# One attention phase in another order on all its engines, with splits and fills one turn later and other PSUM banks for the units

## The chip, the core and the metric

The program runs on one core of one Trainium2 chip. The core has five engines that run their own instruction streams side by side: PE (TensorE, matmuls), DVE (VectorE), ACT (ScalarE), POOL (GpSimd) and SP (SyncE, which here issues DMAs). They order their work between them by semaphores. The metric is the device time of the whole program in microseconds (us); lower is better.

## What is computed

The program computes four layers in a row on x of shape (32, 256, 128): a retention layer, a mixture of experts, an attention layer, and a routed decoder block. The change touches the third, and the bookkeeping of x around it:

```
# 16 heads of 8 values each, 32 sequences of 256 tokens
def _L1_attn_ref(hidden_states, Wq, bq, Wk, bk, Wv, bv, Wo, bo):
    q = (hidden_states @ Wq.T + bq).reshape(b, s, HEADS, HEAD_DIM)
    k = (hidden_states @ Wk.T + bk).reshape(b, s, HEADS, HEAD_DIM)
    v = (hidden_states @ Wv.T + bv).reshape(b, s, HEADS, HEAD_DIM)
    q = q * SCALE
    scores = jnp.einsum('bqhd,bkhd->bhqk', q, k)
    probs = jax.nn.softmax(scores.astype(jnp.float32), axis=-1)
    out = jnp.einsum('bhqk,bkhd->bqhd', probs, v).reshape(b, s, d)
    return out @ Wo.T + bo
...
x = x + _L1_attn_ref(_layernorm(x), ...)
```

## The kernel before

**The phase.** `attention_phase` (L1008) works on the 32 sequences one after the other, as a software pipeline. Each engine has its own list of steps with a lag each, handed to `pipeline` (L55): in turn n of that engine, a step with lag g works on sequence n - g. Rounds 0 to 9 are written out, rounds 10 to 31 run in a hardware loop whose body holds two turns, and the rest is written out again. Engines stay in step only by semaphores, so turn n of one engine need not lie at the same time as turn n of another.

**One sequence.** DVE takes statistics of x (`stats_of`, `moments`), POOL makes the factors from them (`inv_std`), ACT normalises (`norm`), PE transposes h (`transpose_h`) and projects q and k (`project_qk`, L1546), ACT copies them out of PSUM (`copy_qk`). To keep f32 precision with bf16 matmuls, POOL splits q and k into three bf16 parts each: `split_qk(0)` and `split_qk(1)`, four instructions each (L1234), every one waiting for the one before. SP stores the parts (`store_parts`, four DMAs) and reads them back into the stacks of one half of the heads (`fill(0)`, `fill(1)`, two DMAs each). PE then computes scores twice. `for_maximum(j)` (m0 to m7, L1460) writes a unit of 4 heads x 128 queries x 256 keys into one of three PSUM slots of two banks each, and DVE takes the row maxima from there (`maximum(j)`, L1319). POOL splits the maxima (`split_max(half)`, four small instructions), PE transposes them (`transpose_max`, L1528), ACT copies them (`copy_maxT`), and SP puts them below the queries (`give_max(half)`). `for_exponential(j)` (e0 to e7, L1476) computes the transposed scores less the maximum into a slot, and ACT takes the exponential (`exponential(j)`, L1406). `values(g)` (L1491) multiplies with v. Then come `copy_o`, `by_token` (L1539), `normalise`, `transpose_o`, `output`, `add_y`, and a second set of statistics with `inv_std3`, `norm3`, `weigh`, `add_up` and `store_out` for the next layer. `pad_v`, `bias` and `add_given` are further steps of POOL.

**What sets the order.** The lists of steps are written by hand, one for each engine. `UNITS` names the 16 units in PE's order, with their lag and slot; before PE writes a slot it waits until DVE or ACT has read the unit that was there (`free_slot`). `TURNS` gives the order in which eight small products share the one bank `ps_misc` (v, oT, y, max1, hT, token, qk, max0): each waits until the one before it is read (`misc_free`).

The lists before, in short: POOL `inv_std3 8, bias 5, inv_std 1, weigh 9, split_max(0) 4, add_given 0, pad_v 4, split_qk(0) 2, split_qk(1) 2, split_max(1) 4`; PE begins its turn with e4 and `values(1)`, and m and e units stand mostly in pairs.

## Time and profile before

| | us |
|---|---|
| median of 3 runs | 1094.35 (1092.17 to 1096.04) |
| the profiled execution, device time | 1095.34 |
| its span, first to last instruction | 1093.6 |
| mean granted TensorE clock | 0.944 of 2.4 GHz |

The time of an execution is 1.74 us more than the span of its trace, for what lies around the instructions. The attention phase takes about 458 to 988 us of the span. Its steady part is a row of turns of some 15 us, one for each sequence; the length of a turn is read from the distance between two starts of the same line, for instance L1539, which runs once a turn. In the trace, "idle before <-releaser" names what ended an engine's wait.

### The profile page before, as it was taken

The numbers are of one execution on the slowest core, as the hardware profiler recorded it, in microseconds if no ns is written. First come the engines' busy times: TensorE is split into PE (matmuls) and PEld (weight loads), VectorE is DVE, ScalarE is ACT, GpSimd is POOL, SyncE is SP. The second block draws the span as 40 slices with busy tenths as digits, with TensorE's granted clock in tenths as the row PEclk, the third lists the DMA queues.
The fourth block names the chain that finished last, engine by engine and source line by source line (L and its number), as shares of the span: only waits on it lengthen the run. The fifth ranks groups of instructions, "written<-read, shape, count | busy, mean of one in ns | idle before, by whom it ended". The sixth has DMA issues, their size and how long they took to land. (4 is left out here: it accounts for less than half of the span.)

```text
span 1093.6 us, 31502 instructions
## 1 busy us (share of the span) xinstructions
PE 978.4 (89%) x9858; PEld 715.5 (65%) x9858; DVE 710.5 (65%) x1509; ACT 642.1 (59%) x1320; POOL 707.5 (65%) x1531
## 2 busy tenths in 40 slices
PE   6999999699989999359999999999999999973776
PEld 5888888489956766235766666666666666642554
DVE  5777777685534444235777888777887778735752
ACT  4666766412223443115788888888888788762552
POOL 4666676467735555456688888888888888635003
PEclk9999999799989999756999999999999999996988
DMA  8500000131123332363344444344444344302000
GB/s 321 246 0 0 0 0 0 40 106 54 50 72 82 84 81 66 92 192 92 112 118 138 120 133 125 117 120 135 115 131 120 112 134 122 112 16 65 12 3 20
DMA packets 84095, 99.99 MB, mean 91 GB/s; under 512 B 10590, under 2 KB 68158, under 8 KB 83646
## 3 DMA queue, kind: packets, MB, share of 16 engines
q1 hardware_dynamic: 78782, 87.97, 27.0%
q0 software_dynamic: 5248, 11.15, 3.2%
q8 instruction: 41, 0.67, 0.3%
q14 instruction: 24, 0.20, 0.1%
HBM read 61.78 MB, written 36.47 MB: 90 GB/s over the span
## 5 line engine op out<-in xcount | busy, mean ns | idle before, releaser
L1319 DVE TENSOR_REDUCE a_neg_max<-a_slot 128x4 f32<-128x1024 f32 x256 | 301.6, 1220 | 89.8 <-PE a_slot L1460 88.2
L1406 ACT ACTIVATE a_pT<-a_slot 128x1024 f32<-128x1024 f32 x256 | 255.6, 1026 | 16.1 <-PE a_slot L1476 14.5
L1476 PE MATMUL a_slot<-a_q_stack,a_k_stack 75*128 75x256 bf16 x1024 | 156.7, 276 | 3.9 <-issue 1.7
L1460 PE MATMUL a_slot<-a_k_stack,a_q_stack 72*128 72x256 bf16 x1024 | 149.8, 281 | 9.0 <-DMA a_k_stack<-part_dram 6.9
L1491 PE MATMUL a_ps_o<-a_pT,a_v_pad 128*32 128x256 f32 x2048 | 138.1, 387 | 0.0
L1460 PEld LDWEIGHTS a_slot<-a_k_stack,a_q_stack 72*128 72x128 bf16 x1024 | 93.5, 100 | 50.9 <-issue 22.0
L702 POOL DMA_INDIRECT y_rows<-m_total,m_token x80 | 76.6, 957 | 67.2 <-ACT m_total L855 53.3
L1476 PEld LDWEIGHTS a_slot<-a_q_stack,a_k_stack 75*128 75x128 bf16 x1024 | 91.7, 98 | 34.4 <-DVE a_neg_max L1319 10.1
L325 DVE TENSOR_TENSOR r_score<-ps_score,r_decay 128x512 f32<-128x512 f32 x128 | 81.5, 678 | 10.1 <-PE ps_score L477 10.0
L1491 PEld LDWEIGHTS a_ps_o<-a_pT,a_v_pad 128*32 128x32 f32 x2048 | 53.6, 109 | 48.4 <-issue 26.3
L695 POOL DMA_INDIRECT sorted_in<-h,m_slot x64 | 63.9, 998 | 26.1 <-issue 18.6
L804 DVE TENSOR_TENSOR m_hidden_e<-m_gate_e,m_banks 128x512 f32<-128x512 f32 x40 | 27.5, 687 | 77.4 <-ACT m_gate_e L850 77.4
L934 PE MATMUL m_banks<-expert_up,m_xeT 128*128 x160 | 77.4, 607 | 0.0
L885 PE MATMUL m_banks<-h2T,shared_up 128*128 (+1 forms) x256 | 61.9, 386 | 2.2 <-DVE m_hidden L751 1.9
L380 ACT ACTIVATE r_h<-x,r_shift,r_rstd 128x128 f32 (+1 forms) x128 | 56.7, 498 | 9.3 <-POOL r_shift L252 9.3
L835 ACT ACTIVATE m_gate<-m_banks 128x512 f32<-128x512 f32 x32 | 19.1, 597 | 66.7 <-PE m_banks L885 66.7
L850 ACT ACTIVATE m_gate_e<-m_banks 128x512 f32<-128x512 f32 x40 | 23.9, 597 | 55.3 <-PE m_banks L934 55.3
L885 PEld LDWEIGHTS m_banks<-h2T,shared_up 128*128 128x128 f32 x256 | 47.2, 194 | 8.8 <-issue 3.4
L1234 POOL TENSOR_TENSOR a_part<-a_qk,a_zeros 128x256 bf16<-128x256 f32 x64 | 39.1, 611 | 16.6 <-ACT a_qk L1392 14.1
L250 POOL TENSOR_TENSOR r_rstd<-r_ve,r_half 128x2 f32<-128x2 f32 x64 | 45.3, 707 | 6.0 <-POOL r_minus_mean L247 1.9
L1234 POOL TENSOR_TENSOR a_part<-a_rest,a_part 128x256 bf16<-128x256 f32 x64 | 42.9, 671 | 5.0
L1234 POOL TENSOR_TENSOR a_rest<-a_qk,a_part 128x256 f32<-128x256 f32 x64 | 42.8, 669 | 5.0
(292 smaller groups left out, 2132.4 us busy)
## 6 DMA issues: line engine op xcount, KB each, us to landing
a_q_stack<-part_dram SPq DMA_DIRECT2D x64, 288.0 KB
a_k_stack<-part_dram SPq DMA_DIRECT2D x64, 288.0 KB
part_dram<-a_part SPq DMA_DIRECT2D x64, 192.0 KB, 2.7
sorted_in<-h SPq DMA_DIRECT2D x10, 528.0 KB, 14.0
m_xe<-sorted_in SPq DMA_DIRECT2D x40, 132.0 KB, 2.3
expert_up<-in_eu_dram SPq DMA_DIRECT2D x1, 4096.0 KB, 25.7
part_dram<-a_part SPq DMA_DIRECT2D x64, 64.0 KB, 3.5
out_dram<-e_x_plus_h SPq DMA_DIRECT2D x32, 128.0 KB, 1.8
```

The lines of the kernel that those rows point to most:

```text
L325: nc.vector.tensor_tensor(score[:, p, tile], ps_score[tile][:], own, ALU.mult).then_inc(score_done, 1)
L380: ins = nc.scalar.activation(h[:, p, t], x_sb[:, s * TPS + t, :], ACT.Identity, bias=shift[:, p, t:t + 1], scale=rstd[:, p, t:t + 1])
L695: nc.gpsimd.indirect_dma_start(sorted_in, bass.IndirectOffsetOnAxis(ap=slot[:, t:t + 1], axis=0), h2_all[:, t, :], None).then_inc(scattere ...
L702: nc.gpsimd.indirect_dma_start(y_rows, bass.IndirectOffsetOnAxis(ap=token[:, at:at + 1], axis=0), ye[:, t % RING, j], None).then_inc(store ...
L885: ins = nc.tensor.matmul(bank[2 * which + p][:, f * S:(f + 1) * S], shared_up[:, which, f], h2T_all[:, bass.ds(s * S, S)], start=True, sto ...
L934: ins = nc.tensor.matmul(bank[PAIR * (p % 2) + j], xeT[:, p % 2, j], w_up[:, expert[j]], start=True, stop=True)
L1234: nc.gpsimd.tensor_tensor(to, a, b, op).then_inc(steps, 1)
L1319: nc.vector.tensor_reduce(neg_max[:, p, half, t, g * UNIT:(g + 1) * UNIT], slots[SLOT_OF["m", j]][:], AX.X, ALU.max, negate=True).then_inc ...
L1406: nc.scalar.activation(pT[:, j % PT_RING], slots[SLOT_OF["e", j]][:], ACT.Exp).then_inc(e_read, 1)
L1460: ins = nc.tensor.matmul(slots[SLOT_OF["m", j]][:, q], q_stack[0:QK_ROWS, p, half, head, t * P:(t + 1) * P], k_stack[0:QK_ROWS, p, half, h ...
L1476: ins = nc.tensor.matmul(slots[SLOT_OF["e", j]][:, q], k_stack[0:EXP_ROWS, p, half, head, t * P:(t + 1) * P], q_stack[0:EXP_ROWS, p, half, ...
L1491: ins = nc.tensor.matmul(ps_o[q * APAD:(q + 1) * APAD, g // 2], v_pad[:, p, t, g * UNIT + q], pT[:, (2 * g + t) % PT_RING, q], start=g % 2 ...
```

## The change

All five lists and the tables `UNITS` and `TURNS` are rewritten. Lines below L1296 have numbers 2 or 3 higher in the changed kernel. No arithmetic step is added or removed.

- On PE the m and e units alternate, and the turn begins with e6. Every unit has its slot from the new `UNITS`.
- On POOL `split_qk` goes from lag 2 to 3, `split_max` from 4 to 5, `inv_std` from 1 to 2; `split_max(0)` stands first and `inv_std` stands between the two `split_qk`.
- On SP `store_parts` goes from lag 1 to 3, the fills from 2 to 3 and 4, and the list begins with `fill(1)`.
- On DVE the maxima m0 to m6 go from lag 3 to 4, `moments` from lag 0 to 1 and behind the fifth maximum; `given_added` waits for two semaphores more.
- On ACT exponentials and copies stand in a new order, with `norm3` at the end (lag 6, from 7).

```diff
-UNITS = (("e", 4, 5, 0), ("e", 5, 5, 2), ("m", 6, 4, 1), ("m", 7, 4, 0), ("e", 6, 5, 2), ("e", 7, 5, 1),
-         ("m", 0, 3, 2), ("m", 1, 3, 1), ("e", 0, 4, 0), ("e", 1, 4, 2), ("m", 2, 3, 0), ("m", 3, 3, 1),
-         ("e", 2, 4, 2), ("e", 3, 4, 0), ("m", 4, 3, 1), ("m", 5, 3, 2))
+UNITS = (("e", 6, 5, 2), ("m", 7, 4, 0), ("e", 7, 5, 1), ("m", 0, 3, 2), ("e", 0, 4, 1), ("m", 1, 3, 0),
+         ("e", 1, 4, 2), ("m", 2, 3, 1), ("e", 2, 4, 0), ("m", 3, 3, 2), ("e", 3, 4, 1), ("m", 4, 3, 0),
+         ("m", 5, 3, 2), ("e", 4, 4, 1), ("m", 6, 3, 0), ("e", 5, 4, 1))
...
-            pipeline(sp, [(give_max(1), 4), (store_out, 9), (fill(0), 2), (give_max(0), 3), (fill(1), 2),
-                          (store_parts, 1)], B, ROUNDS)
+            pipeline(sp, [(fill(1), 4), (store_parts, 3), (store_out, 9), (give_max(1), 5),
+                          (fill(0), 3), (give_max(0), 4)], B, ROUNDS)
...
-            pipeline(pool, [(inv_std3, 8), (bias, 5), (inv_std, 1), (weigh, 9), (split_max(0), 4), (add_given, 0),
-                            (pad_v, 4), (split_qk(0), 2), (split_qk(1), 2), (split_max(1), 4)], B, ROUNDS)
+            pipeline(pool, [(split_max(0), 5), (weigh, 9), (add_given, 0), (split_qk(0), 3), (inv_std, 2),
+                            (split_max(1), 5), (split_qk(1), 3), (bias, 5), (pad_v, 4), (inv_std3, 8)], B, ROUNDS)
...
             def given_added(s, p, r):
+                after(dve, stats_done, s - 1)
+                after(dve, ve_done, 2 * (s - 2))
                 after(dve, added, s + 1)
...
-            pipeline(dve, [(given_added, 0), (maximum(7), 4), (add_up, 9), (stats_of, 0), (moments3, 7),
-                           (maximum(0), 3), (maximum(1), 3), (settle, 0), (add_y, 6), (moments, 0),
-                           (maximum(2), 3), (maximum(3), 3), (normalise, 5), (y_is_added, 6), (maximum(4), 3),
-                           (maximum(5), 3), (stats3_of, 6), (maximum(6), 3), (settle3, 6), (preset_v_pad, 0)], B, ROUNDS)
+            pipeline(dve, [(given_added, 0), (maximum(0), 4), (add_up, 9), (add_y, 7), (maximum(1), 4),
+                           (maximum(2), 4), (moments3, 8), (stats_of, 0), (y_is_added, 7), (maximum(3), 4),
+                           (normalise, 6), (maximum(4), 4), (moments, 1), (stats3_of, 7), (maximum(5), 4),
+                           (settle3, 7), (maximum(6), 4), (settle, 0), (maximum(7), 4), (preset_v_pad, 0)], B, ROUNDS)
...
-            pipeline(act, [(norm3, 7), (exponential(3), 4), (copy_qk, 1), (exponential(4), 4), (copy_maxT(0), 3),
-                           (exponential(5), 4), (copy_v, 1), (copy_o(0), 4), (exponential(6), 4),
-                           (exponential(7), 4), (copy_oT, 5), (norm, 0), (exponential(0), 3), (exponential(1), 3),
-                           (copy_o(1), 4), (copy_maxT(1), 3), (copy_hT, 0), (exponential(2), 3)], B, ROUNDS)
+            pipeline(act, [(copy_qk, 1), (exponential(4), 4), (copy_maxT(0), 3), (copy_o(0), 4),
+                           (exponential(5), 4), (exponential(6), 4), (copy_v, 1), (exponential(7), 4),
+                           (copy_oT, 5), (exponential(0), 3), (norm, 0), (copy_maxT(1), 3), (exponential(1), 3),
+                           (copy_o(1), 4), (copy_hT, 0), (exponential(2), 3), (exponential(3), 3),
+                           (norm3, 6)], B, ROUNDS)
...
-            TURNS = (("max0", 4, maxT_copied, 2, 0), ("v", 2, v_copied, 1, 0), ("oT", 6, oT_copied, 1, 0),
-                     ("y", 6, y_added, 1, 0), ("max1", 4, maxT_copied, 2, 1), ("hT", 1, hT_copied, 1, 0),
-                     ("token", 5, otok_copied, 1, 0), ("qk", 1, qk_copied, 1, 0))
+            TURNS = (("v", 2, v_copied, 1, 0), ("oT", 6, oT_copied, 1, 0), ("y", 6, y_added, 1, 0),
+                     ("max1", 4, maxT_copied, 2, 1), ("hT", 1, hT_copied, 1, 0), ("token", 5, otok_copied, 1, 0),
+                     ("qk", 1, qk_copied, 1, 0), ("max0", 3, maxT_copied, 2, 0))
...
-            pipeline(pe, [(for_exponential(4), 5), (values(1), 5), (transpose_max(0), 4), (for_exponential(5), 5),
-                          (for_maximum(6), 4), (for_maximum(7), 4), (project_v, 2), (for_exponential(6), 5),
-                          (for_exponential(7), 5), (values(2), 5), (for_maximum(0), 3), (transpose_o, 6),
-                          (for_maximum(1), 3), (for_exponential(0), 4), (output, 6), (for_exponential(1), 4),
-                          (values(3), 5), (for_maximum(2), 3), (transpose_max(1), 4), (for_maximum(3), 3),
-                          (for_exponential(2), 4), (transpose_h, 1), (values(0), 4), (by_token, 5),
-                          (for_exponential(3), 4), (for_maximum(4), 3), (for_maximum(5), 3),
-                          (project_qk, 1)], B, ROUNDS)
+            pipeline(pe, [(for_exponential(6), 5), (project_v, 2), (for_maximum(7), 4), (for_exponential(7), 5),
+                          (values(2), 5), (for_maximum(0), 3), (transpose_o, 6), (for_exponential(0), 4),
+                          (for_maximum(1), 3), (output, 6), (for_exponential(1), 4), (for_maximum(2), 3),
+                          (transpose_max(1), 4), (values(3), 5), (transpose_h, 1), (for_exponential(2), 4),
+                          (for_maximum(3), 3), (for_exponential(3), 4), (by_token, 5), (values(0), 4),
+                          (for_maximum(4), 3), (project_qk, 1), (for_maximum(5), 3), (for_exponential(4), 4),
+                          (for_maximum(6), 3), (transpose_max(0), 3), (values(1), 4),
+                          (for_exponential(5), 4)], B, ROUNDS)

```

**POOL, in the hardware loop.** What stands there after the second `split_qk` and at the loop's jump. Rows without a tile (REGISTER_ALU, ISA, branches) are instructions that POOL's sequencer handles: they compute addresses and wait values. Semaphores are printed under the name of their first owner: r_k_tok_done counts the steps of `split_qk`, r_stats2_part those of `split_max`, r_x1_done is `maxT_done`, r_stats2_done is `m_read`. Before:

```order
L1234 TENSOR_TENSOR a_part<-a_rest,a_part 128x256 [waits r_k_tok_done]
L45 REGISTER_ALU
L45 REGISTER_ALU [waits r_k_tok_done]
L45 REGISTER_ALU [waits r_x1_done]
L1234 TENSOR_TENSOR a_max_part<-a_neg_max,a_zeros 128x2x8 [waits r_stats2_done]
...
L1234 TENSOR_TENSOR a_max_part<-a_max_rest,a_max_part 128x2x8 [waits r_stats2_part]
L67 REGISTER_ALU [waits r_stats2_part]
L67 COMPARE_AND_BRANCH
```

Now:

```order
L1234 TENSOR_TENSOR a_max_part<-a_max_rest,a_max_part 128x2x8 [waits r_stats2_part]
L1234 TENSOR_TENSOR a_part<-a_qk,a_zeros 128x256 [waits r_qk_done,r_stats2_part]
...
L1234 TENSOR_TENSOR a_part<-a_rest,a_part 128x256 [waits r_k_tok_done]
L45 REGISTER_ALU
L1205 ISA [waits r_shift1_done,r_k_tok_done]
L1205 TENSOR_TENSOR x<-x,a_bo 128x256
...
L1220 TENSOR_TENSOR e_shift<-e_minus_mean,e_rstd 128x2 [waits e_rstd_done]
L67 REGISTER_ALU
L67 COMPARE_AND_BRANCH
```

The second maximum split moved from behind the second `split_qk` to ahead of it, and the jump now follows `inv_std3` in place of a split.

**SP, in the hardware loop.** The stores of the parts (L1143, L1147) and the DMA that gives the maxima of the second half (L1166; r_ve2_done is `maxT_copied`). Before:

```order
L1147 DMA part_dram<-a_part 64x6x256 [waits r_k_tok_done]
L1147 DMA part_dram<-a_part 64x6x256
L45 REGISTER_ALU
L1166 DMA a_q_stack<-a_max_T 3x8x256 [waits r_ve2_done]
L45 REGISTER_ALU
L1173 ISA [waits e_out_done]
L1173 DMA out_0_dram<-e_x_plus_h 128x2x128
```

Now:

```order
L1147 DMA part_dram<-a_part 64x6x256 [waits r_k_tok_done]
L1147 DMA part_dram<-a_part 64x6x256
L45 REGISTER_ALU
L1173 ISA [waits e_out_done]
L1173 DMA out_0_dram<-e_x_plus_h 128x2x128
L45 REGISTER_ALU
L1166 DMA a_q_stack<-a_max_T 3x8x256 [waits r_ve2_done]
```

The output store now goes ahead of the maxima; how long the first row waits depends on POOL, whose second `split_qk` now ends later relative to `transpose_max(1)`.

**PE, the start of a turn.** The units m6, m7, e6, e7, `values(2)`, m0, m1 with their slots, before:

```order
L1460 MATMUL a_slot1<-a_k_stack,a_q_stack 128x256 x4
L1460 MATMUL a_slot0<-a_k_stack,a_q_stack 128x256 x4
L1552 MATMUL a_ps_misc<-a_wv,a_hT 128x128 x2
L1476 MATMUL a_slot2<-a_q_stack,a_k_stack 128x256 x4
L1476 MATMUL a_slot1<-a_q_stack,a_k_stack 128x256 x4
L1491 MATMUL a_ps_o<-a_pT,a_v_pad 32x256 x8
L1460 MATMUL a_slot2<-a_k_stack,a_q_stack 128x256 x4
```

Now, from e6 on (e6, v, m7, e7, `values(2)`, m0, e0):

```order
L1479 MATMUL a_slot2<-a_q_stack,a_k_stack 128x256 x4
L1555 MATMUL a_ps_misc<-a_wv,a_hT 128x128 x2
L1463 MATMUL a_slot0<-a_k_stack,a_q_stack 128x256 x4
L1479 MATMUL a_slot1<-a_q_stack,a_k_stack 128x256 x4
L1494 MATMUL a_ps_o<-a_pT,a_v_pad 32x256 x8
L1463 MATMUL a_slot2<-a_k_stack,a_q_stack 128x256 x4
L1479 MATMUL a_slot1<-a_q_stack,a_k_stack 128x256 x4
```

Before, e7 took slot 1 after m6 with only m7, v and e6 between. Now slot 1 goes from e7 to e0 with `values(2)` and m0 between, and m6 hands slot 0 to m7.

## Rows read from the trace of the kernel before

**Rows 1.** Stretch of 80 us: PE, PEld, DVE, ACT, POOL busy; clock; DMA share; GB/s.

```profile
640.00:720.00 80.00, 79.30 (x812) 54.78 (x809) 63.41 (x107) 65.23 (x113) 68.12 (x161) 1.00 0.43 124
```

**Rows 2.** Timeline of PE, one line (L1539) of five turns: start us, us, line.

```profile
521.47 0.66 PE L1539 MATMUL a_ps_misc<-ident,a_oT_pad 128*128 128x128 f32 x4
536.34 0.66 PE L1539 MATMUL a_ps_misc<-ident,a_oT_pad 128*128 128x128 f32 x4
...
865.78 0.66 PE L1539 MATMUL a_ps_misc<-ident,a_oT_pad 128*128 128x128 f32 x4
880.55 0.66 PE L1539 MATMUL a_ps_misc<-ident,a_oT_pad 128*128 128x128 f32 x4
895.92 0.66 PE L1539 MATMUL a_ps_misc<-ident,a_oT_pad 128*128 128x128 f32 x4
```

**Rows 3.** Timeline of POOL, its last wait and its next one at `split_qk(0)`.

```profile
569.90 0.61 POOL L1234 TENSOR_TENSOR a_part<-a_qk,a_zeros 128x256 bf16<-128x256 f32 x1 [0.56 <-ACT a_qk L1392]
...
929.51 0.61 POOL L1234 TENSOR_TENSOR a_part<-a_qk,a_zeros 128x256 bf16<-128x256 f32 x1 [1.99 <-ACT a_qk L1392]
```

**Rows 4.** Timeline of POOL: end of `split_max(1)`, start of `inv_std3`, then `bias`.

```profile
546.79 0.22 POOL L1234 TENSOR_TENSOR a_max_part<-a_max_rest,a_max_part 128x16 bf16<-128x16 f32 x1
547.09 0.20 POOL L1212 TENSOR_TENSOR e_ve<-e_mv,a_eps 128x2 f32<-128x2 f32 x1
...
863.09 0.22 POOL L1234 TENSOR_TENSOR a_max_part<-a_max_rest,a_max_part 128x16 bf16<-128x16 f32 x1
863.53 0.19 POOL L1212 TENSOR_TENSOR e_ve<-e_mv,a_eps 128x2 f32<-128x2 f32 x1 [0.22 <-POOL a_max_part L1234]
...
864.88 0.74 POOL L1205 TENSOR_TENSOR x<-x,a_bo 128x256 f32 x1
...
877.86 0.22 POOL L1234 TENSOR_TENSOR a_max_part<-a_max_rest,a_max_part 128x16 bf16<-128x16 f32 x1
878.66 0.19 POOL L1212 TENSOR_TENSOR e_ve<-e_mv,a_eps 128x2 f32<-128x2 f32 x1 [0.58 <-POOL a_max_part L1234]
...
880.18 0.73 POOL L1205 TENSOR_TENSOR x<-x,a_bo 128x256 f32 x1
```

**Rows 5.** Timeline of PE: e6 and e7 (x8), `values(2)`, m0; m2 and `transpose_max(1)`.

```profile
856.80 1.21 PE L1476 MATMUL a_slot<-a_q_stack,a_k_stack 75*128 75x256 bf16 x8
857.94 1.07 PE L1491 MATMUL a_ps_o<-a_pT,a_v_pad 128*32 128x256 f32 x16
858.95 0.61 PE L1460 MATMUL a_slot<-a_k_stack,a_q_stack 72*128 72x256 bf16 x4
859.39 0.38 PE L1560 MATMUL a_ps_misc<-ident,a_o_tok 128*128 128x128 f32 x2
...
862.53 0.61 PE L1460 MATMUL a_slot<-a_k_stack,a_q_stack 72*128 72x256 bf16 x4
863.36 0.28 PE L1528 MATMUL a_ps_misc<-a_ident_b,a_max_part 128*24 128x128 bf16 x2 [0.22 <-POOL a_max_part L1234]
```

**Rows 6.** Timeline of the phase's start: first factors, first padding, first units, first projections.

```profile
460.17 0.20 POOL L1212 TENSOR_TENSOR a_ve<-a_mv,a_eps 128x2 f32<-128x2 f32 x1 [0.90 <-DVE a_mv L1310]
460.25 0.91 DVE L1292 MEMSET a_v_pad<- 128x1024 f32 x1 [0.16 <-issue]
...
481.91 2.74 PE L1460 MATMUL a_slot<-a_k_stack,a_q_stack 72*128 72x256 bf16 x12 [6.93 <-DMA a_k_stack<-part_dram]
...
507.12 1.06 PE L1545 MATMUL a_ps_misc<-a_hT,a_wq 128*128 128x256 f32 x2
```

**Rows 7.** Timeline of SP's queue, one turn: start us, us of issuing.

```profile
862.00 1.24 SPq L1147 DMA_DIRECT2D part_dram<-a_part  x2
...
865.20 0.40 SPq L1173 DMA_DIRECT2D out_dram<-e_x_plus_h  x1
```

**Rows 8.** DMA issues on the page: KB each, median us from issue to landing.

```profile
part_dram<-a_part SPq DMA_DIRECT2D x64, 192.0 KB, 2.7
...
out_dram<-e_x_plus_h SPq DMA_DIRECT2D x32, 128.0 KB, 1.8
```

## What the change will do to the time

> **What bounds the kernel now.** I read the timelines of PE and POOL over the attention phase first, since all edits lie there. In an 80 us stretch of the steady part PE is busy 79.30 us at full clock, and POOL 68.12, DVE 63.41 and ACT 65.23 [rows 1]. That looks like a PE bound. The starts of L1539 tell more: while the rounds are written out a turn takes 536.34 - 521.47 = 14.87 us; in the loop turns of 880.55 - 865.78 = 14.77 and 895.92 - 880.55 = 15.37 alternate, 30.14 a pair, and by_token(25) starts 895.92 - 521.47 = 374.45 us after by_token(0) [rows 2]. What makes one turn of two longer is POOL. Its 68.12 busy us leave out the short gaps in which a step waits for POOL's own step before it, and those lie on POOL's path. Its last wait for another engine in the steady part, 0.56 us, ends at 569.90; the next comparable one ends at 929.51 [rows 3]. Between them POOL runs its 30.14 us of steps a pair back to back, and PE waits where it needs a maximum split: `transpose_max(1)` starts 0.83 us after m2, a unit of 0.44, released by POOL [rows 5].
>
> Two parts of POOL's 30.14 us depend on the order. From the last instruction of `split_max(1)` to the next step it is 0.30 us in the written-out rounds (546.79 to 547.09), but 0.44 in the loop (863.09 to 863.53) [rows 4]: there the wait for the split stands on a register instruction, and the real one comes 0.14 to 0.15 later. Before, such places are split_max(0) to add_given, the second split_qk to split_max(1), and split_max(1) to inv_std3: three a turn. Across the loop's jump the same distance is 0.80 (877.86 to 878.66) [rows 4], so the jump costs 0.36 a pair.
>
> PE alone would need less. A unit is 0.44, `values` 1.00; e6 with e7 take 857.94 - 856.80 = 1.14 in place of 0.88, since e7 waits 0.26 for the maximum of m6 in its slot [rows 5]. 14.77 less this and less the two short waits at `transpose_max` leaves some 14.45 us of PE's own work a turn. So an order that only helps PE is worth little in the loop: POOL sets its length.
>
> **PE's turn in the new order.** The instructions are the same. `values` was followed once a turn by the small `transpose_max(0)` and is now always followed by a full product; I add 0.12 (estimate, some tenth of its 1.00) and get 14.57. e7's wait for m6 goes. New tight places: e1 takes m0's slot two units after m0's copy could begin, m2 that of e0, e0 that of e7. Laid out by the durations above, they come out at 0 to 0.1 us each; I take 0.1 a turn in all, so 14.67, with 14.57 and 15.1 as ends (0.1 to 0.2 at each of three places). In the loop both figures lie under POOL's half pair, so they cost nothing there unless they pass it.
>
> **POOL's turn in the new order (the main term).** In the loop's second half the wait stands on a register instruction only at split_max(0) to weigh and at the second split_qk to bias: two places in place of three, -0.15. split_qk(1) after split_max(1), and inv_std after split_qk(0), carry their waits themselves. The inv_std to split_max(1) step gets two register instructions, +0.05. In the first half of the pair it stays at three places, with one more register instruction at two of them, +0.15. The jump now follows a step whose end nobody waits for, as 0.36 again or 0.05 more. After the jump, inv_std3 used to take 880.18 - 878.66 = 1.52 against 864.88 - 863.53 = 1.35 in the other turn [rows 4], and inv_std, as I take it, 0.1 more; both had a second register instruction ahead of a wait, which now stands there once at most: -0.27. Sum: -0.15 + 0.05 + 0.15 - 0.27 = -0.22 a pair, so 29.92. The split steps themselves keep their length. Bounds: +0.3 if every one of the four drained places pays 0.15 in both halves (11 pairs: +3.3 us), and down to PE's own pair of 29.34, under which it cannot matter (11 x -0.8 = -8.8 us). I stay near the middle because the 0.15 and the 0.36 are read at just such places.
>
> A rule of the Trainium skill bears on the jump. The rows show 0.36 us more across it [rows 4]. The page "Advanced Engine Details and Errata", section Control Flow Timing, gives about 108 ns for a compare-and-branch. By that price the jump would be worth 0.1 us a pair wherever it stood, 1.2 us in all; the trace shows three times as much, and the sum goes by the trace.
>
> **The start.** `moments` of sequence 0 now stands one DVE turn later, behind the statistics of sequence 1 and the 0.91 us memset of v_pad [rows 6]; the first inv_std on POOL, at 460.17 before, moves by about 0.9 + 0.1 + 0.9 = 1.9 us. The two splits of sequence 0 have inv_std(1) between them, which was not between them before, but add_given moves too; the second store and the fill follow 1.9 us later, and m0, at 481.91 before [rows 6], comes at about 483.8. From there on PE at half clock, DVE and the fill of sequence 1 share the path. Before, PE waited in pieces for DVE and for copies there; in the new order m units stand one behind the other without `transpose_max(0)` between, and part of that wait goes. Laid out, project_qk(3) comes at 507 to 509, against 507.12 [rows 6]. I take +0.7, with -0.5 and +3.0 as ends.
>
> **Written-out turns, loop and end.** From by_token(0) on: three turns at PE's pace until POOL's first `weigh` fills its turn, 3 x 14.67 = 44.0; then 11 pairs at 29.92 = 329.1. In the new order POOL may slide by about 0.75 us against PE before PE waits (from 1.2 us behind by_token to 1.95), which PE gains once. 44.0 + 329.1 - 0.75 = 372.35, against 374.45: -2.1. After the loop POOL has no add_given and falls off the path; turns then go at 14.7 where one still took 15.0: -0.4. The bank changes have no price of their own beyond the places named. The two added waits in `given_added` are for statistics and factors a turn and more old, and nothing is late for them.
>
> **Sum.** +0.7 - 2.1 - 0.4 = -1.8 us. On the profiled execution: span 1093.6 - 1.8 = 1091.8, with 1.74 around it 1093.5. That execution lies 1.0 above the median 1094.35, so the forecast for the median is 1092.6, chance 0.38 (1090 to 1094.5).
>
> **Rivals.**
>
> *A, slower: the maxima of the second half wait in SP's queue.* give_max(1) now stands behind the four stores and store_out. From the end of the second split_qk to landing it is 0.1 + 1.24 (two stores) + 0.1 + 0.40 + 0.1 + 1.8 = 3.75 us [rows 7, 8], with 1.8 the landing of the small output store; with the 2.7 of the part stores it is 4.65. From there e4 to m3's maximum in the next turn is some 12.5 us of PE and DVE, and from that maximum through POOL to the end of the second split_qk 12.0, with 1.3 of register places and jump in a pair (estimates: 14.57 and POOL's half pair, less the steps that lie outside). That is a loop of 29.6 us over two turns with the short landing and 30.5 with the long one. Beyond 2.1 us it passes POOL's 29.92 and sets the pair: 11 x 0.6 = +6.4, so 1099. Against it: 12 KB in 24 rows is the smallest transfer there. Chance 0.20.
>
> [...]
>
> *B, faster: POOL falls off the path.* If the moved steps hide the register instructions wholly, POOL's pair falls to PE's 29.34 and no further: 0.58 x 11 = 6.4 us more than forecast, 1086.2. For it: POOL's own steps without those places are 14.77 - 3 x 0.15 = 14.3 a turn before. Against: the jump and two places remain. Chance 0.20.
>
> *C, nothing: the order changes no length.* POOL keeps 30.14 us a pair, since every step is still there, and slots and banks act on PE, which waits for POOL anyway. Then only the start stays: 1094.35 + 0.7 to + 1.9, about 1095.3. Chance 0.22.
>
> **How the numbers follow.** About 0.3% (3.3 us) is what a measurement can tell here: faster is under 1091.1, slower over 1097.6. Faster: B and the lower edge of the forecast, 0.20 + 0.08 = 0.28. Slower: A and a start at its upper end, 0.20 + 0.02 = 0.22. The rest, 0.50, lies within. The range runs from B's 1086.0 to just past A's 1099, 1099.5, which leaves a tenth on either side.
>
> **What would show it.** In the profile after: m0 some 2 us later than 481.91; L1539 in the loop at pairs of 29.9 (B: 29.4, C: 30.1, A: 30.5 with PE waiting ahead of e4 and no wait of POOL's missing); POOL without a wait for another engine through the loop; e7 without its 0.26. The forecast is wrong if POOL shows waits for `m_read` or `qk_copied` in the loop, since then a cycle through PE and DVE, not POOL's own steps, sets the turn.

## The result, and the profile after

| | before | after |
|---|---|---|
| median of 22 runs each, us | 1093.61 (1088.85 to 1097.68) | 1091.13 (1087.74 to 1093.09) |
| ratio to before | | 0.9974, 95% interval 0.9962 to 0.9986 |
| profiled execution, device time, us | 1095.34 | 1088.45 |
| its span, us | 1093.6 | 1086.7 |

The change gained 2.5 us by the medians. The forecast was 1.8 us less than before, and 1092.6 for the median. The two profiled executions lie 6.9 us apart. Some of that is no work of the change: in the trace of after the attention phase begins 0.9 us earlier, at 457.21 (before 458.10), and what follows the last `w_tok` takes 104.1 us against 106.1 (spans less 982.61 and 987.49), in code that the change does not touch. Between the two the stretches below sum to -4.0 us (the first lies inside the second), where the medians of 22 runs say -2.5 (by the interval -1.5 to -4.2). So the rest of this text compares stretches inside the attention phase, each from its own first row. The first product is the first matmul of the phase (L1436 before, L1439 now); by_token(n) is the row of L1539, now L1542, for sequence n; `w_tok` is DVE's last result for the next layer.

| stretch | before, us | after, us | difference | forecast |
|---|---|---|---|---|
| first product of the phase to m0 | 23.81 | 26.07 | +2.3 | +1.9 |
| first product to by_token(0) | 63.37 | 60.89 | -2.5 | +0.7 |
| by_token(0) to by_token(25) | 374.45 | 372.82 | -1.6 | -2.1 |
| by_token(25) to by_token(31) | 82.38 | 80.26 | -2.1 | -0.4, with the next row |
| by_token(31) to the last w_tok | 9.19 | 11.43 | +2.2 | in the row above |

The profile after, in the views that were shown of before. First the timeline of PE (start us, us, line), the line that runs once a turn, now L1542; it answers to [rows 2]:

```profile
518.10 0.60 PE L1542 MATMUL a_ps_misc<-ident,a_oT_pad 128*128 128x128 f32 x4
532.67 0.60 PE L1542 MATMUL a_ps_misc<-ident,a_oT_pad 128*128 128x128 f32 x4
...
890.92 0.60 PE L1542 MATMUL a_ps_misc<-ident,a_oT_pad 128*128 128x128 f32 x4
```

The first turn takes 14.57 us in place of 14.87. In the loop turns of 14.75 and 15.26 alternate, a pair of 30.01 to 30.02 in place of 30.14, and by_token(25) comes 890.92 - 518.10 = 372.82 us after by_token(0).

The timeline of POOL through one pair of the loop, the places where a step ends and the next begins, which answer to [rows 4]:

```profile
833.00 0.20 POOL L1220 TENSOR_TENSOR e_shift<-e_minus_mean,e_rstd 128x2 f32<-128x2 f32 x1
833.55 0.21 POOL L1234 TENSOR_TENSOR a_max_part<-a_neg_max,a_zeros 128x16 bf16<-128x16 f32 x1 [0.36 <-issue]
...
834.43 0.22 POOL L1234 TENSOR_TENSOR a_max_part<-a_max_rest,a_max_part 128x16 bf16<-128x16 f32 x1
835.02 0.72 POOL L1273 TENSOR_TENSOR e_product<-h,d_rw 128x256 f32<-128x256 f32 x1 [0.37 <-POOL a_max_part L1234]
...
839.20 0.68 POOL L1234 TENSOR_TENSOR a_part<-a_rest,a_part 128x256 bf16<-128x256 f32 x1
840.10 0.19 POOL L1212 TENSOR_TENSOR a_ve<-a_mv,a_eps 128x2 f32<-128x2 f32 x1 [0.22 <-POOL a_part L1234]
...
844.78 0.67 POOL L1234 TENSOR_TENSOR a_part<-a_rest,a_part 128x256 bf16<-128x256 f32 x1
845.73 0.73 POOL L1205 TENSOR_TENSOR x<-x,a_bo 128x256 f32 x1 [0.29 <-POOL a_part L1234]
...
848.35 0.19 POOL L1220 TENSOR_TENSOR e_shift<-e_minus_mean,e_rstd 128x2 f32<-128x2 f32 x1
848.53 0.21 POOL L1234 TENSOR_TENSOR a_max_part<-a_neg_max,a_zeros 128x16 bf16<-128x16 f32 x1
...
849.41 0.22 POOL L1234 TENSOR_TENSOR a_max_part<-a_max_rest,a_max_part 128x16 bf16<-128x16 f32 x1
849.90 0.73 POOL L1273 TENSOR_TENSOR e_product<-h,d_rw 128x256 f32<-128x256 f32 x1 [0.27 <-POOL a_max_part L1234]
...
859.52 0.67 POOL L1234 TENSOR_TENSOR a_part<-a_rest,a_part 128x256 bf16<-128x256 f32 x1
860.39 0.74 POOL L1205 TENSOR_TENSOR x<-x,a_bo 128x256 f32 x1 [0.20 <-POOL a_part L1234]
...
863.56 0.21 POOL L1234 TENSOR_TENSOR a_max_part<-a_neg_max,a_zeros 128x16 bf16<-128x16 f32 x1 [0.36 <-issue]
```

863.56 - 833.55 = 30.01 is the pair, and every wait in it is for POOL itself or for "issue" (time in which the engine waited for nothing that the profile shows): the bracket never names another engine. Across the jump a `shift` is followed by the next step after 0.55, and without the jump after 0.18, so the jump costs 0.37.

The timeline of PE in the loop, m5, e4, and then e7 with `values(2)`, which answer to [rows 5]:

```profile
848.50 0.60 PE L1463 MATMUL a_slot<-a_k_stack,a_q_stack 72*128 72x256 bf16 x4
849.86 0.61 PE L1479 MATMUL a_slot<-a_q_stack,a_k_stack 75*128 75x256 bf16 x4 [0.76 <-DMA a_q_stack<-a_max_T]
...
853.68 0.60 PE L1479 MATMUL a_slot<-a_q_stack,a_k_stack 75*128 75x256 bf16 x4
854.21 1.07 PE L1494 MATMUL a_ps_o<-a_pT,a_v_pad 128*32 128x256 f32 x16
```

e7 no longer waits: e6 to e7 to `values(2)` has no wait in it, and `values` starts 0.53 after e7. But e4 waits 0.76 us in one turn and 0.28 in the other for the DMA that brings the maxima, which is where rival A had put its wait.

### The profile page after: what moved, and what is told of

The parts are those of the page before. It is cut to its first block and busy times, and to the rows that moved or that the text cites. A ratio compares the mean times of both kernels' runs of the same rounds, so it can differ in the third digit from the quotient of the medians.

```text
span 1086.7 us, 31598 instructions
## 1 busy us (share of the span) xinstructions
PE 961.3 (88%) x9858; PEld 714.6 (66%) x9858; DVE 707.5 (65%) x1509; ACT 641.3 (59%) x1320; POOL 707.8 (65%) x1531
## 5 line engine op out<-in xcount | busy, mean ns | idle before, releaser
L1321 DVE TENSOR_REDUCE a_neg_max<-a_slot 128x4 f32<-128x1024 f32 x256 | 307.1, 1218 | 117.1 <-PE a_slot L1463 111.0
L1463 PE MATMUL a_slot<-a_k_stack,a_q_stack 72*128 72x256 bf16 x1024 | 159.2, 280 | 5.3 <-DMA a_k_stack<-part_dram 4.8
L1479 PE MATMUL a_slot<-a_q_stack,a_k_stack 75*128 75x256 bf16 x1024 | 151.2, 275 | 11.9 <-DMA a_q_stack<-a_max_T 10.2
L1494 PE MATMUL a_ps_o<-a_pT,a_v_pad 128*32 128x256 f32 x2048 | 141.7, 386 | 0.0
L1494 PEld LDWEIGHTS a_ps_o<-a_pT,a_v_pad 128*32 128x32 f32 x2048 | 64.9, 109 | 27.4 <-issue 13.0
L1426 ACT ACTIVATE h<-x,e_shift,e_rstd (+1 forms) x64 | 28.0, 484 | 38.0 <-POOL e_shift L1220 37.8
```

Of the source, the lines that this page charges most:

```text
L1321: nc.vector.tensor_reduce(neg_max[:, p, half, t, g * UNIT:(g + 1) * UNIT], slots[SLOT_OF["m", j]][:], AX.X, ALU.max, negate=True).then_inc ...
L1463: ins = nc.tensor.matmul(slots[SLOT_OF["m", j]][:, q], q_stack[0:QK_ROWS, p, half, head, t * P:(t + 1) * P], k_stack[0:QK_ROWS, p, half, h ...
L1479: ins = nc.tensor.matmul(slots[SLOT_OF["e", j]][:, q], k_stack[0:EXP_ROWS, p, half, head, t * P:(t + 1) * P], q_stack[0:EXP_ROWS, p, half, ...
L1494: ins = nc.tensor.matmul(ps_o[q * APAD:(q + 1) * APAD, g // 2], v_pad[:, p, t, g * UNIT + q], pT[:, (2 * g + t) % PT_RING, q], start=g % 2 ...
```

## Experiments

The chips differ in what lies ahead of and behind the attention phase, so each kernel was timed beside the kernel before on its own chip, and ratios are to that. The names begin with a for the changed kernel and b for the kernel before. The first four kernels ran on one chip, where the median of before was 1119.16 us. For the next four it was 1092.14, for the last three 1092.75. The numbers in brackets are 95% intervals; the changed kernel itself had 0.9974 on its chip.

**1. Is the pair POOL's, and what does the hardware loop cost?** 30 turns written out instead of 10, in the changed order and in the order before:

```diff
-ROUNDS = 10
+ROUNDS = 30
```

> The changed kernel with 30 turns written out and one pair left in the hardware loop (ROUNDS = 30). The work is the same; jump, register instructions and the waits they carry are gone from 22 of 32 turns. Theory (POOL bounds the loop by its instructions plus 0.37 us at the jump and 0.15 to 0.35 us at each place where a drained wait is carried by a register instruction): every turn goes at the pace of the written-out turns of the trace, 14.57 to 14.81 us against 15.01 on average in the loop, so 11 pairs save 0.4 to 0.9 us each: 5 to 9 us faster than the changed kernel, 1082 to 1086 us. Rival 1 (the written-out code costs fetching on some engine): no gain or a loss of some us, with new idle time that no semaphore ends. Rival 2 (PE's order bounds the pair, not POOL): pair stays at 30.0 and the time within 1 us.

> The kernel before with 30 turns written out and one pair left in the hardware loop. Theory (POOL bounds, in both kernels): written-out turns of the trace took 14.87, 14.87, 14.80, 14.80 us on POOL's pace, against 15.07 in the loop; 11 pairs save 0.4 to 0.6 us each: 4 to 7 us faster than the kernel before (1087 to 1090 us). With the changed kernel's twin this gives what the order is worth once the loop's own costs are gone: the changed order ahead by 3 to 6 us, since its first turns went 14.57 and PE's own work is 14.6. Rival (the order is worth only what it saved in the register waits): the two written-out kernels are within 1 us of each other outside the start.

Measured: a_rounds30 0.9946 [0.992, 0.9972], b_rounds30 0.9998 [0.9965, 1.0032]. By_token(0) to by_token(25) takes 367.02 us (372.82 in the loop) and 372.00 (374.45). The timelines of PE, three turns each, first a_rounds30, then b_rounds30:

```profile
803.65 0.60 PE L1542 MATMUL a_ps_misc<-ident,a_oT_pad 128*128 128x128 f32 x4
818.32 0.60 PE L1542 MATMUL a_ps_misc<-ident,a_oT_pad 128*128 128x128 f32 x4
832.96 0.60 PE L1542 MATMUL a_ps_misc<-ident,a_oT_pad 128*128 128x128 f32 x4
```

```profile
806.57 0.66 PE L1539 MATMUL a_ps_misc<-ident,a_oT_pad 128*128 128x128 f32 x4
821.43 0.66 PE L1539 MATMUL a_ps_misc<-ident,a_oT_pad 128*128 128x128 f32 x4
836.30 0.65 PE L1539 MATMUL a_ps_misc<-ident,a_oT_pad 128*128 128x128 f32 x4
```

Turns of 14.64 and 14.86 us. And what each engine did in the same 150 us (columns as in [rows 1]) in a_rounds30, b_rounds30 and the changed kernel:

```profile
700.00:850.00 150.00, 149.92 (x1555) 106.30 (x1553) 120.82 (x209) 124.80 (x216) 131.06 (x311) 1.00 0.46 130
```

```profile
700.00:850.00 150.00, 150.00 (x1532) 102.68 (x1530) 120.66 (x202) 122.03 (x211) 129.07 (x304) 1.00 0.44 128
```

```profile
700.00:850.00 150.00, 145.00 (x1522) 102.76 (x1521) 118.49 (x201) 121.53 (x211) 127.76 (x301) 1.00 0.44 124
```

Outside the loop PE is busy all but 0.08 us of 150, and POOL waits for others: 0.25 to 0.27 us a turn for DVE's maxima in the changed order, 0.50 a turn for ACT's q and k in the old one. Inside it PE has 5.0 us of gaps in ten turns and POOL has none for others. The times moved the way of the theory, but less: in the changed order 3 us by the ratios and 5.8 by the traces, where 5 to 9 were expected; the ratio of the changed kernel is from another chip, and a_addup, on this one, has 372.75 in its trace too, so the traces are the better reading. In the order before the trace gives 2.4 us where 4 to 7 were expected, and the timing alone, with its interval of 0.7% of 1119 us, shows nothing.

**2. Is it the queue of SP (rival A)?** give_max(1) ahead of the stores (the rest of the list is as it was):

```diff
-            pipeline(sp, [(fill(1), 4), (store_parts, 3), (store_out, 9), (give_max(1), 5),
+            pipeline(sp, [(fill(1), 4), (give_max(1), 5), (store_parts, 3), (store_out, 9),
```

> The changed kernel with give_max(1) moved ahead of store_parts and store_out in SyncE's queue. In the changed kernel e4 waits 0.76 and 0.28 us per pair for the transfer of give_max(1). Theory (POOL bounds the loop, e4's wait only shows POOL's lateness): the pair stays at 30.0 us, e4's wait or another wait on POOL's values takes the same time, and the kernel stays within 1 us of the changed one. Rival (the transfer of the maxima is late because of what stands ahead of it in the queue, so that the queue bounds): the wait goes, the pair falls by 0.3 to 0.7 us, and the kernel is 3 to 8 us faster.

Measured: 0.9995 [0.9964, 1.0026], pair 30.02 to 30.03 us. The time alone, with an interval of some 3.5 us to either side, could not tell the 1 us of the expectation; the pair can. The timelines of PE where it waits now, and of ACT ahead of that:

```profile
850.47 0.22 PE L1531 MATMUL a_ps_misc<-a_ident_b,a_max_part 128*24 128x128 bf16 x1 [0.28 <-ACT a_qk L1394]
...
865.84 0.22 PE L1531 MATMUL a_ps_misc<-a_ident_b,a_max_part 128*24 128x128 bf16 x1 [0.90 <-ACT a_qk L1394]
...
864.09 0.88 ACT L1426 ACTIVATE h<-x,e_shift,e_rstd  x2 [2.21 <-POOL e_shift L1220]
864.88 0.45 ACT L1393 ACTIVATE a_qk<-a_ps_misc,a_bq_scaled 128x256 f32<-128x256 f32 x1
```

e4 waits no more, and PE now loses 0.28 + 0.90 us a pair at `transpose_max(0)`. Its bank is freed by ACT's copy of q and k, and that stood behind `norm3`, which had waited 2.21 us for POOL's factors: the wait leads back to POOL again. Before the edit PE lost 0.76 + 0.28 at e4. The wait moved, the pair stayed: rival A's wait is real as a place and has no price. The edit costs something in the first turns (15.14, 15.55 and 15.55 where the changed kernel had 14.63, 14.81 and 14.33), 0.7 us in all from by_token(0) to by_token(25).

**3. More and less work for POOL.** a_poolmore adds one operation to each turn; a_poolless and b_poolless do `bias` for 8 columns of one tile and leave out the rest of it, so their output is not the layer's. The edit:

```diff
-                nc.gpsimd.tensor_tensor(some, some, bo[:].unsqueeze(1).to_broadcast([P, TPS, D]), ALU.add
+                part_of = x_sb[:, bass.ds(s * TPS, 1), 0:8]
+                nc.gpsimd.tensor_tensor(part_of, part_of, bo[:, 0:8].unsqueeze(1).to_broadcast([P, 1, 8]), ALU.add
```

and a_poolmore has this one, where `spare` is a buffer that nobody reads:

```diff
+                after(pool, spare_done, s)
+                nc.gpsimd.tensor_tensor(spare[:], router[:].unsqueeze(1).to_broadcast([P, TPS, D]), bo[:].unsqueeze(1).to_broadcast([P, TPS, D]), ALU.add).then_inc(spare_done, 1)
```

> The changed kernel with one more operation of GpSimd in each turn, of the size of the sum in weigh (0.69 us from start to start), into a buffer of its own that nobody reads. Theory (GpSimd bounds every turn of the loop, with no slack): the pair rises by 1.3 to 1.6 us to 31.3 to 31.6, and in the written-out turns, where 14.6 was TensorE's pace, to 15.2 to 15.4 a turn; 19 to 23 us slower than the changed kernel. Rival (TensorE bounds and GpSimd only follows close behind): the pair rises by less than 0.7.

> The changed kernel with bias on GpSimd done for 8 columns of one tile only (the rest of the bias of the attention's output is left out), which takes 0.5 to 0.6 us of GpSimd's work out of each turn; loop of the hardware as in the changed kernel. Theory (GpSimd bounds the loop at 30.02 us a pair, TensorE's own pair is 29.3 as in a_rounds30): the pair falls to 29.3 to 29.6, GpSimd waits for others by some 0.5 us a pair, the kernel is 4 to 7 us faster than the changed one. Rival (TensorE pays for the loop itself, and that is why the pair is 30.0 in the loop and 29.3 outside): the pair stays above 29.8 although GpSimd has time to spare.

> The kernel before with the same part of bias left out on GpSimd. Theory (TensorE's own pair in the order before is 29.73, as in b_rounds30, and GpSimd's 30.14 hides it): the pair falls to 29.7 to 29.9 and no further, 3 to 5 us faster than the kernel before; against its twin a_poolless this is the worth of TensorE's new order, 0.4 us a pair, that GpSimd hides in the change itself. Rival (what I reckoned in the prediction, TensorE's own work of 14.45 us a turn before the change): the pair falls to 29.1 to 29.4, no slower than the changed order. The start gives a second look at the order before: by_token(0) comes 63.4 us after the phase's first product in the kernel before and 60.2 in b_rounds30, which have the same code there; if the difference is when the granted clock rises (52 and 46 us after it), this run shows one or the other, with the rise to match.

Measured: a_poolmore 1.0119 [1.0097, 1.0141], a_poolless 0.9867 [0.9848, 0.9887], b_poolless 0.9952 [0.9935, 0.9969]. The timelines of PE, three turns of the loop each, of a_poolmore, a_poolless and b_poolless:

```profile
812.42 0.60 PE L1546 MATMUL a_ps_misc<-ident,a_oT_pad 128*128 128x128 f32 x4
828.17 0.60 PE L1546 MATMUL a_ps_misc<-ident,a_oT_pad 128*128 128x128 f32 x4
843.79 0.60 PE L1546 MATMUL a_ps_misc<-ident,a_oT_pad 128*128 128x128 f32 x4
```

```profile
810.80 0.60 PE L1543 MATMUL a_ps_misc<-ident,a_oT_pad 128*128 128x128 f32 x4
825.47 0.60 PE L1543 MATMUL a_ps_misc<-ident,a_oT_pad 128*128 128x128 f32 x4
839.79 0.60 PE L1543 MATMUL a_ps_misc<-ident,a_oT_pad 128*128 128x128 f32 x4
```

```profile
803.86 0.66 PE L1540 MATMUL a_ps_misc<-ident,a_oT_pad 128*128 128x128 f32 x4
818.59 0.66 PE L1540 MATMUL a_ps_misc<-ident,a_oT_pad 128*128 128x128 f32 x4
833.35 0.66 PE L1540 MATMUL a_ps_misc<-ident,a_oT_pad 128*128 128x128 f32 x4
```

Pairs of 31.37, 28.99 and 29.49 us. With 2 x 0.69 us more on POOL the pair grows by 1.35: POOL has no slack in it. With 0.53 us a turn less (`bias` to `pad_v` takes 0.16 where it took 0.69) it shrinks in both orders, by 1.0 in the changed one and 0.65 in the old one. In b_poolless PE is busy for the whole of 150 us and POOL waits for ACT, so 29.49 is PE's own pair in the order before. In a_poolless the pair shrinks by all that POOL lost, POOL still shows no wait for another engine, and PE still waits for the maxima: e4 starts 0.76 us after m5 in one turn and 0.43 in the other. POOL still sets the pair there, and PE's own pair in the new order is 28.99 or less. The new order is thus worth 0.5 us a pair or more on PE, of which the change could bank 0.12. My expectations were wrong in two places. The written-out turns (14.64 and 14.86) are not PE's floor: the loop's turns go below them once POOL lets them, so the pairs came out under the 29.3 to 29.6 and 29.7 to 29.9 expected, and a_poolless gained 11.7 us on the changed kernel by the ratios where 4 to 7 were expected. And I counted POOL's extra operation in the first written-out turns of a_poolmore too, where it does not run yet, so 15.8 us of loss (0.0145 of 1092) stand against the 19 to 23 expected.

**4. Where do the last turns give it back?** Four kernels. First one step of VectorE's list moved:

```diff
-            pipeline(dve, [(given_added, 0), (maximum(0), 4), (add_up, 9), (add_y, 7), (maximum(1), 4),
-                           (maximum(2), 4), (moments3, 8), (stats_of, 0), (y_is_added, 7), (maximum(3), 4),
+            pipeline(dve, [(given_added, 0), (maximum(0), 4), (add_y, 7), (maximum(1), 4),
+                           (maximum(2), 4), (moments3, 8), (add_up, 9), (stats_of, 0), (y_is_added, 7), (maximum(3), 4),
```

> The changed kernel with one step moved in VectorE's list: add_up (lag 9) stands behind moments3 (lag 8) instead of ahead of add_y. Theory (the tail gives back what the last turns won): in the changed kernel add_up(30) waits for POOL's product at 977.98 and keeps moments3(31) from starting at 975.9, where its statistics were done; by_token(31) to the last w_tok takes 11.43 us there against 9.19 us in the kernel before. Without that wait ahead of it this stretch becomes 8.5 to 9.5 us and the kernel 2 to 3 us faster than the changed one (about 1088.5 by the medians, 0.995 of the kernel before), with the loop's pair of turns still at 30.0 us. Rival (the last turns are bound by POOL's own queue, where weigh(30) and inv_std3(31) follow one another whatever VectorE does): the stretch stays above 11 us and the time within 0.5 us of the changed kernel.

Measured: 0.9977 [0.9952, 1.0002], and 11.84 us from by_token(31) to the last `w_tok`. The theory fell. `moments3(31)` did come earlier, at +5.6 us after by_token(31) instead of +8.0, but POOL came to `inv_std3(31)` no sooner, at +8.7 instead of +8.3, because `weigh(30)` stood ahead of it.

So the next kernel undid that order on POOL. It has 30 turns written out (twin: a_rounds30) and `weigh` at lag 10; `add_up` and `store_out`, which follow it, go to lag 10 too (not shown):

```diff
-            pipeline(pool, [(split_max(0), 5), (weigh, 9), (add_given, 0), (split_qk(0), 3), (inv_std, 2),
+            pipeline(pool, [(split_max(0), 5), (weigh, 10), (add_given, 0), (split_qk(0), 3), (inv_std, 2),
```

> The changed kernel with 30 turns written out (as in a_rounds30) and weigh, add_up and store_out one turn later (lag 10 instead of 9); the twin is a_rounds30. Theory (the tail waits on GpSimd's order, not on VectorE's): the changed order puts weigh(30) ahead of inv_std3(31), so that each of the last turns goes round POOL to ScalarE's norm3 and back, 3.75 us a time; by_token(31) to the last w_tok takes 11.49 us in a_rounds30 and 9.30 in b_rounds30, where inv_std3(31) comes first. With weigh one turn later, inv_std3(31) comes ahead of weigh(30) again: 9.2 to 9.9 us, so 1.6 to 2.3 us faster than a_rounds30, with turns of 14.65 us as there. Rival (the stretch is bound by PE's and VectorE's last steps, which weigh doesn't touch): it stays above 11 us. Should hold of the time: 0.992 to 0.994 of the kernel before.

Measured: 0.9936 [0.9917, 0.9954]. The stretch took 10.76 us against 11.49 in the twin: 0.73 us less, where 1.6 to 2.3 were expected. `inv_std3(30)` still started 4.45 us after by_token(31), 2.59 in the kernel before. The delay was there ahead of anything that the two edits had touched.

The third kernel goes at that start, with POOL's list left as changed and `moments3` at its lag of 8:

```diff
-            pipeline(dve, [(given_added, 0), (maximum(0), 4), (add_up, 9), (add_y, 7), (maximum(1), 4),
-                           (maximum(2), 4), (moments3, 8), (stats_of, 0), (y_is_added, 7), (maximum(3), 4),
+            pipeline(dve, [(given_added, 0), (maximum(0), 4), (moments3, 8), (add_up, 9), (add_y, 7), (maximum(1), 4),
+                           (maximum(2), 4), (stats_of, 0), (y_is_added, 7), (maximum(3), 4),
```

> The changed kernel with moments3 moved in VectorE's list to stand ahead of add_up and add_y; GpSimd's list as in the changed kernel. Theory (VectorE's order starts the long last chain late): in the changed kernel moments3(30) waits in VectorE's queue behind add_y(31), so that inv_std3(30) begins 4.4 us after by_token(31) against 2.6 us in the kernel before. With moments3 ahead of add_y it begins 2.3 to 2.8 us after it, weigh(30) at 4.9, inv_std3(31) at 6.3, and the last w_tok at 9.3 to 9.8 instead of 11.43: 1.6 to 2.1 us faster than the changed kernel, 0.9950 to 0.9965 of the kernel before, the loop's pair at 30.0 as there. Rival (GpSimd's order alone sets the tail): above 10.8. The start once more in the changed order: by_token(0) at 60.9 to 61.2 after the phase's first product if the granted clock rises 48 us after it.

The fourth puts the other half, `weigh` ahead of `inv_std3` on POOL, into the kernel before:

```diff
-            pipeline(pool, [(inv_std3, 8), (bias, 5), (inv_std, 1), (weigh, 9), (split_max(0), 4), (add_given, 0),
+            pipeline(pool, [(weigh, 9), (inv_std3, 8), (bias, 5), (inv_std, 1), (split_max(0), 4), (add_given, 0),
```

> The kernel before with one part of the change alone: in GpSimd's list weigh stands ahead of inv_std3, as it does in the changed one. Theory (each such order costs one round from GpSimd to ScalarE's norm3 and back, but only 0.5 to 1 us of it is left where moments3 comes early): inv_std3(31) moves from 5.7 to 6.5 us after by_token(31), the last w_tok from 9.19 to 9.6 to 10.1. Rival (GpSimd's order was the whole of the 2.2 us): 11 or more. The loop's pair stays within 0.15 of 30.14, as the same work and about the same waits are there. Start, third look at the order before on another day: by_token(0) at 63.4 after the phase's first product with the clock's rise at 52, or at 60.2 with the rise at 46.

Measured: a_moments3 0.9952 [0.9934, 0.9969], b_weighfirst 0.9993 [0.9974, 1.0013]. Each stretch, by its rows of by_token(31) on PE, the last factors on POOL and the last `w_tok` on DVE; first the changed kernel, then a_moments3, then b_weighfirst:

```profile
971.18 0.66 PE L1542 MATMUL a_ps_misc<-ident,a_oT_pad 128*128 128x128 f32 x4 [0.49 <-ACT a_oT_pad L1415]
...
979.46 0.19 POOL L1212 TENSOR_TENSOR e_ve<-e_mv,a_eps 128x2 f32<-128x2 f32 x1
...
982.61 0.42 DVE L1360 TENSOR_REDUCE w_tok<-e_product 128x2 f32<-128x256 f32 x1 [3.22 <-POOL e_product L1273]
```

```profile
972.47 0.66 PE L1542 MATMUL a_ps_misc<-ident,a_oT_pad 128*128 128x128 f32 x4 [0.49 <-ACT a_oT_pad L1415]
...
978.55 0.20 POOL L1212 TENSOR_TENSOR e_ve<-e_mv,a_eps 128x2 f32<-128x2 f32 x1
...
981.70 0.42 DVE L1360 TENSOR_REDUCE w_tok<-e_product 128x2 f32<-128x256 f32 x1 [3.33 <-POOL e_product L1273]
```

```profile
978.72 0.66 PE L1539 MATMUL a_ps_misc<-ident,a_oT_pad 128*128 128x128 f32 x4 [0.49 <-ACT a_oT_pad L1413]
...
985.06 0.20 POOL L1212 TENSOR_TENSOR e_ve<-e_mv,a_eps 128x2 f32<-128x2 f32 x1
...
988.21 0.42 DVE L1358 TENSOR_REDUCE w_tok<-e_product 128x2 f32<-128x256 f32 x1 [3.33 <-POOL e_product L1273]
```

11.43, 9.23 and 9.49 us, against 9.19 in the kernel before; `inv_std3(31)` starts at +8.28, +6.08, +6.34 and +5.71. So the 2.2 us are VectorE's: the change put `moments3` behind `add_y`, where it had stood ahead of it, and `add_y` waits for the last thing that PE makes. The lag is not the cause: `add_y` and `moments3` both moved by one turn, and a_moments3 keeps the new lag. POOL's order alone, put into the kernel before, costs 0.3. b_weighfirst kept its pair near 30.1 as expected.

**5. The version that the runs point to.** a_tail has 30 turns written out, `weigh`, `add_up` and `store_out` at lag 10, and `moments3` ahead of `add_up` and `add_y`.

> The version that the runs so far point to: the changed kernel with 30 turns written out, weigh, add_up and store_out one turn later, and moments3 ahead of add_y. In a_weigh10 the last w_tok came 10.76 us after by_token(31), because moments3(30) and moments3(31) stood behind add_y(31) and add_up(29). Theory: inv_std3(30) at +2.4, weigh(29) behind it, inv_std3(31) at +5.3, weigh(30) and weigh(31) in a row from +6.6, the last w_tok at 8.7 to 9.3: 1.5 to 2.1 us less than a_weigh10, and 0.991 to 0.993 of the kernel before in all. Rival (the last steps are bound by the chain of PE, ScalarE and VectorE that ends with add_y(31), 4 us behind by_token(31), plus 6.4 us of what follows): above 10.2.

Measured: 1086.4 us, 0.9931 [0.991, 0.9953], the lowest ratio of those that compute everything. The last stretch took 8.92 us, as expected. But its turns took 14.69 in place of 14.64 us, 368.44 us from by_token(0) to by_token(25) against 367.29 in a_weigh10, so 1.2 of the 1.8 us went back into the turns. Its interval overlaps those of a_rounds30, a_weigh10 and a_moments3; which of these is best isn't shown, that all four beat the kernel before is.

## Why the prediction was right, and where not

**POOL bounds the loop: right, and shown.** POOL's pair has no wait for another engine after the change either; the pair follows POOL's work up and down (31.37 and 28.99 us), and does not follow the queue of SP.

**POOL's pair, forecast 29.92, measured 30.01 to 30.02.** The places were right, and the gain was forecast at nearly twice its size (0.22 for 0.12 to 0.13) by an error of 0.1 us. Outside the loop the steps stand 0.29 and 0.75 us apart at these places. In the loop they stand 0.59 and 0.49 apart at split_max(0) to `weigh`, 0.95 and 0.87 at the second split_qk to `bias`, 0.90 at split_qk(0) to `inv_std`: +0.30, +0.20, +0.20, +0.12 and +0.15, together 0.97. The forecast had 0.90 for them (five times 0.15, and 0.15 for further register instructions). The jump costs 0.37 for 0.36. The 0.27 after the jump went wholly: no step of `inv_std` or `inv_std3` is longer there now. In the kernel before, the six drained places come to 0.87 by their rows where the forecast took 0.90. The 0.05 for inv_std to split_max(1) did not show; they stand 0.17 apart, as `e_shift` and the next split do. These are hundredths, as small as the rows can tell; no single term carries the 0.1.

**PE's own turn: the parts were right, the sum went by the wrong side.** Before, 14.45 and the 0.26 of e7 make 14.71; b_poolless shows 14.74. For the new order I added 0.12 for a full product behind `values` and 0.1 for tight places, 14.67; a_poolless shows 14.50 or less, and its quicker turn is 14.33. This cost nothing in the forecast, since POOL lay above both. It made rival B's floor of 29.34 too high.

**The start: m0 right (+2.3 for +1.9), the term wrong (-2.5 for +0.7).** The forecast followed the waits as far as project_qk(3) and held the clock fixed. Both went wrong. The forecast had project_qk(3) 0 to 2 us later; it came 0.6 us earlier, 48.46 us after the phase's first product where it was 49.02 [rows 6]:

```profile
505.67 0.60 PE L1548 MATMUL a_ps_misc<-a_hT,a_wq 128*128 128x256 f32 x2
```

From there to by_token(0) it took 12.43 us where it had been 14.35. The granted clock rises from 0.50 to 1.00 (1.2 to 2.4 GHz) in this stretch, and it rose sooner. The granted clock is the number ahead of the last two in these rows of two microseconds each, of the kernel before and of the changed one:

```profile
508.00:510.00 2.00, 2.00 (x11) 1.10 (x13) 0.87 (x1) 0.91 (x3) 0.01 (x1) 0.50 0.70 246
510.00:512.00 2.00, 2.00 (x26) 1.26 (x22) 0.00 (x0) 1.54 (x3) 1.84 (x3) 0.93 0.01 4
```

```profile
503.00:505.00 2.00, 2.00 (x18) 0.60 (x16) 0.63 (x1) 1.02 (x1) 0.98 (x5) 0.50 0.17 18
505.00:507.00 2.00, 2.00 (x17) 1.60 (x14) 1.13 (x1) 0.26 (x1) 0.61 (x1) 0.88 0.66 209
```

It rose 52 us after the phase's first product before and 48 us after it now, so 3.2 us behind project_qk(3) ran at half clock before and none now. That is up to 1.6 us of the 2.5 (estimate: half of 3.2). Behind m0, PE's waits up to by_token(0) sum to 1.74 us where they were 3.32; m0 itself is 2.3 later. The rest of the stretch wasn't taken apart. b_poolless and b_weighfirst have the start of before and show the same, 52 us and by_token(0) at 63.53 and 63.46. The five other changed-order kernels on these chips (a_weigh10, a_poolless, a_poolmore, a_moments3, a_tail) show the rise at 48 and by_token(0) at 60.8 to 61.2. So on these chips some 2.4 us go with the new order, and the earlier rise with them; that the order brings the rise about isn't shown. On the chip of the first series b_rounds30 has the start of before too, its rise at 46 us, and by_token(0) at 60.19; there the changed order had the rise at 47 to 49 us and by_token(0) at 59.5 to 60.4, and the order was worth next to nothing. Between b_rounds30 and the kernel before by_token(0) differs by 3.2 us. The waits of PE in this stretch agree to 0.01 us but for one, the fill ahead of m0, 6.37 us for 6.93. So 0.6 us are that DMA's, and 2.6 go with the time of the rise. What makes it come earlier in the one case and not in the other stays open.

**Turns and end: the loop's -2.1 was -1.6, the end's -0.4 was +0.1, in a way not foreseen.** The forecast looked only at PE's and POOL's turns there. PE gained 2.1 us from by_token(25) to by_token(31). Then the last chain, which no later turn hides, lost 2.2: `moments3(30)` waited behind `add_y(31)`. I had looked at the place of `moments3` nowhere, since in the steady part nobody waits for it.

**The rivals.** A (1099): its wait exists, 1.04 us a pair ahead of e4, with its DMA as releaser, and costs nothing while POOL is later still; a_givefirst shows that. B (1086.2): POOL did not fall off; taking POOL's work away gave pairs of 28.99, below the floor of 29.34 that B had. C: the pair would have stayed at 30.14, and it did not, but at 0.12 instead of 0.22 C was nearer than I had it. The time itself was hit partly by luck, by errors that offset each other: the start brought -2.5 where +0.7 was forecast, and the loop and the end 0.5 us less each than forecast (-1.6 for -2.1, +0.1 for -0.4). In the traces the stretches sum to -4.0 us, more than twice the -1.8 forecast; only the medians, at -2.5, are near it.

**The jump.** It costs 0.37 us a pair on POOL after the change too. The Trainium skill ("Advanced Engine Details and Errata", Control Flow Timing) gives some 108 ns for a compare-and-branch; as the price of the whole jump that is too small by a factor of three. At the jump there stands a register instruction beside the branch, and no run here takes the two apart. The written-out twins show what the loop costs, jump and registers together, as far as PE does not hide it: by the most frequent turn 30.02 - 29.28 = 0.74 us a pair in the changed order, and 30.14 - 29.73 = 0.41 in the old one.

## What to carry to other kernels

In the steady turns of a pipeline that is bound by one engine, a new order is worth only what it takes out of that engine's own gaps: 0.12 us a pair was banked here and 0.5 or more of PE's hidden behind POOL, and a run with a little of POOL's work left out tells both numbers at once. Read the drain of a pipeline apart from its steady turns, since a step that nobody waits for inside can, put behind another, be the first link of the last chain. And where a short body is bound by an engine with many small instructions, count what its hardware loop costs in registers and jumps before reordering it.

## What the runs showed that I had not expected

- Written-out code was not PE's fastest: 14.64 us a turn outside the loop against turns of 14.33 inside it once POOL had less to do (changed order), and 14.86 against 14.74 (old order). The difference lies in small distances, as 0.60 against 0.45 ahead of `project_qk` in the changed order. Its cause wasn't sought and is open.
- At the places where a register instruction of POOL carries the wait for its own last step, the next step comes 0.12 to 0.30 us later than in written-out code, not at one price; the dearest of them is the first behind the jump.
- With the same code, and waits of PE that differ by 0.6 us in one DMA, the clock rose at 46 us on one chip (one trace) and at 52 on others (three traces).
